# Making the KAN weights inside the forward transform stage instead of in a block of their own in front

## The reference

```
xn = group_norm(x, 32 groups)                      # no scale, no shift
x1 = spectral_conv2d(xn, w1, w2)                   # rfft2, 16 x 16 low modes of both corners mixed over channels, irfft2
y  = x1 + conv_w . xn + conv_b                     # 1x1 convolution
y  = kan_linear(y, k1_base, k1_spline, k1_scaler)  # per pixel, 64 -> 64 channels
y  = kan_linear(y, k2_base, k2_spline, k2_scaler)
out = x + gelu(y)

kan_linear(v) = silu(v) @ base.T + einsum('nik,oik->no', b_splines(v), spline * scaler[..., None])
```

## Time and profile before

| | us |
|---|---|
| median of 3 runs | 3841.19 (3837.57 to 3843.26) |
| the profiled execution | 3846.3 |
| its span | 3844.5 |
| TensorE busy | 3672.3 (96%) |
| VectorE busy | 3525.7 (92%) |
| ScalarE busy | 3397.2 (88%) |
| mean granted clock of TensorE | 0.984 |

### The profile page before, as it was taken

How to read it: one execution, slowest core, us unless ns; L and a number is a source line. 1 busy time by engine, 2 the same in 40 slices (tenths; PEclk the granted TensorE clock), 3 DMA queues, 4 the chain that set the end, 5 groups by cost and what they waited for, 6 DMA issues and landing times.

```text
span 3844.5 us, 103434 instructions
## 1 busy us (share of the span) xinstructions
PE 3672.3 (96%) x38186; PEld 1791.6 (47%) x38186; DVE 3525.7 (92%) x3959; ACT 3397.2 (88%) x3512; POOL 110.8 (3%) x132
## 2 busy tenths in 40 slices
PE   4995679999999999999999999999999999999998
PEld 2443334444444444444444444444444444444444
DVE  5773269999999999999999999999999999999997
ACT  1551269999999999999999999999999999999996
POOL 0000000000000000000000000000000000000000
PEclk9996899999999999999999999999999999999999
DMA  5999542332233223222322332232223223322321
GB/s 144 290 284 181 172 117 60 71 71 62 62 71 71 58 67 71 65 60 70 71 64 60 71 71 59 65 71 69 58 68 71 65 59 71 71 61 63 71 71 45
DMA packets 327345, 328.77 MB, mean 86 GB/s; under 512 B 87040, under 2 KB 259584, under 8 KB 325248
## 3 DMA queue, kind: packets, MB, share of 16 engines
q1 hardware_dynamic: 304256, 256.74, 24.9%
q0 software_dynamic: 18432, 67.12, 10.8%
q10 hardware_dynamic: 4608, 4.20, 0.3%
HBM read 239.90 MB, written 88.08 MB: 85 GB/s over the span
## 4 chain that ended last, share of the span: by engine, by line
PE 85%; DVE 0%; issue 0%; ACT 0%; POOL 0%; POOLq 0%; ACTq 0%; DVEq 0%
PE l_ps L1068 80%; PE y_ps L1055 3%; PE y_ps L1047 2%; DVE cube2l L944 0%; DVE cube3r L944 0%; ACT above L983 0%; ACT size L994 0%; ACT offset L998 0%; ACT S L987 0%; ACT below L991 0%; DVE cube1r L944 0%; DVE cube1l L944 0%; DVE cube0l L944 0%; ACT L987 0%; DVE cube0r L944 0%
## 5 line engine op out<-in xcount | busy, mean ns | idle before, releaser
L998 ACT ACTIVATE offset<-size 128x1024 f32<-128x1024 f32 x1280 | 1240.4, 1044 | 8.1
L944 DVE SCALAR_TENSOR_TENSOR cube0r<-below,offset 128x1024 f32<-128x1024 f32 x256 | 312.4, 1220 | 57.6 <-ACT offset L998 57.0
L1068 PE MATMUL l_ps<-S,kan_w 64*64 64x512 f32 x2048 | 357.2, 591 | 7.9 <-issue 7.9
L1068 PE MATMUL l_ps<-cube1l,kan_w 64*64 64x512 f32 x2048 | 357.1, 589 | 1.3 <-issue 1.3
L1068 PE MATMUL l_ps<-cube3r,kan_w 64*64 64x512 f32 x2048 | 356.7, 589 | 0.9 <-DVE cube3r L944 0.9
L1068 PE MATMUL l_ps<-cube0r,kan_w 64*64 64x512 f32 x2048 | 356.7, 590 | 0.6 <-DVE cube0r L944 0.6
L1068 PE MATMUL l_ps<-below,kan_w 64*64 64x512 f32 x2048 | 357.0, 591 | 0.0
L1068 PE MATMUL l_ps<-cube3l,kan_w 64*64 64x512 f32 x2048 | 356.7, 589 | 0.1
L1068 PE MATMUL l_ps<-cube2l,kan_w 64*64 64x512 f32 x2048 | 356.7, 589 | 0.1
L1068 PE MATMUL l_ps<-cube4r,kan_w 64*64 64x512 f32 x2048 | 356.7, 589 | 0.1
L1068 PE MATMUL l_ps<-cube4l,kan_w 64*64 64x512 f32 x2048 | 356.7, 589 | 0.1
(11 more groups left out here) (126 smaller groups left out, 6832.8 us busy)
## 6 DMA issues: line engine op xcount, KB each, us to landing
big<-in_x_dram SPq DMA_DIRECT2D x128, 512.0 KB, 7.0
x_ring<-in_x_dram SPq DMA_DIRECT2D x256, 256.0 KB, 4.1
act_out<-in_x_dram POOLq DMA_DIRECT2D x128, 512.0 KB, 6.8
out_dram<-act_out SPq DMA_DIRECT2D x128, 512.0 KB, 2.7
rows_scratch<-rows SPq DMA_DIRECT2D x16, 1024.0 KB, 6.1
rows_t<-rows_scratch SPq DMA_DIRECT2D x512, 32.0 KB, 5.5
big<-in_spec_w_r_dram SPq DMA_DIRECT2D x16, 512.0 KB, 11.3
big<-in_spec_w_i_dram SPq DMA_DIRECT2D x16, 512.0 KB, 11.6
```

The costliest lines, as they stand in the source:

```text
L944: nc.vector.scalar_tensor_tensor(out=cube[q][side][:], in0=distance[layer][:], scalar=EDGE - KNOTS[q], in1=offset[layer][q][:], op0=ALU.mi ...
L998: nc.scalar.activation(offset[layer][q][:], size[layer][:], ACT.Square, bias=-KNOTS[q]).then_inc(offset_ready[layer], 1)
L1068: ins = nc.tensor.matmul(dst[cols, r * MM:(r + 1) * MM], kan_w[layer][rows_, f, :], src[rows_, n * MM:(n + 1) * MM], start=(f == 0), stop= ...
```

## The change

`prepare_weights` is deleted as a block, and its work is done inside `forward`:

- SyncE loads all three tables directly behind group 0 of image 0, then the natural weights of both layers: layer 0 on partitions 0 to 63, layer 1 on 64 to 127, and the 1x1 weights on both halves, and only then groups 1 to 7. Between image 1 and the loop it issues the 1x1 bias, the inverse table and, behind a wait for VectorE, four copies of the KAN bias. In front of the mixing weights it waits for all of these.
- VectorE does the arithmetic (`spline_weights`: the body of the loop over the layers of `prepare_weights`, L244 to L288, without the clearing of `both` and the doubling of `mats`, and with its last two steps linked) once, on 128 partitions for both layers, ahead of the statistics of image 0. The working tiles lie in the third quarter of `big`.
- TensorE turns the 15 matrices (14 and the 1x1 weights) behind image 0, four to a PSUM bank, each twice for the two column halves; ScalarE evicts a bank at a time into one tile `turned_w`, in which the layers are interleaved. `kan_w[l]` and `conv_two` are views of it.
- The first iteration of ScalarE's loop over image pairs is written out.

```diff
-        kan_w = [held(f"kan_w{l}", [P, NF, C]) for l in range(2)]
-        conv_two = held("conv_two", [P, C])
+        turned_w = held("turned_w", [P, NF + 1, 2, C])
+        kan_w = [turned_w[:, 0:NF, l, :] for l in range(2)]
+        conv_two = turned_w[:, NF, 0, :]
...
 def first_half(nc, t):
-    prepare_weights(nc, t)
...
+def spline_weights(nc, dve, w, worked):
...
+    link(nc.vector.tensor_copy(m[:, F_SQUARE, :], bowl))
+    link(nc.vector.tensor_reduce(w["bias"], zero, AX.X, ALU.add))
...
 def forward(nc, t):
+        taken = [0]
+        def early(*shape):
+            n = int(np.prod(shape))
+            part = big[:, 2, taken[0]:taken[0] + n]
+            taken[0] += n
+            assert taken[0] <= C * W
+            return part if len(shape) == 1 else part.rearrange("p (a b) -> p a b", b=shape[1])
+        wide = NB + 2 * PAD
+        kan = {"spline": early(C, NB), "scaler": early(C), "padded": early(C, wide), "both": early(NK, C),
+               "inner": early(4, C), "sums": early(2, C), "mats": early(NF + 1, C), "bias": early(1)}
+        kan["diff"] = [early(C, wide - 1 - k) for k in range(PAD)]
...
+        weights_ps = [ctx.enter_context(nc.psum_tensor(f"weights_ps{i}", [P, 4, 2, C], F32)) for i in range(2)]
+        TURNS = [(f, min(f + 4, NF + 1)) for f in range(0, NF + 1, 4)]
...
         def _(sp):
             sp.dma_start(dft_h_sb[:], t["dft_h"]).then_inc(tables_loaded, 16)
             load(0, 0, 0)
             sp.dma_start(eye[:], t["ident"]).then_inc(tables_loaded, 16)
+            sp.dma_start(dft_w_sb[:], t["dft_w"]).then_inc(tables_loaded, 16)
+            for l, (b_, s_, c_) in enumerate(((t["k1_base"], t["k1_spline"], t["k1_scaler"]),
+                                              (t["k2_base"], t["k2_spline"], t["k2_scaler"]))):
+                own = slice(l * C, (l + 1) * C)
+                sp.dma_start(kan["spline"][own], s_).then_inc(natural_loaded, 16)
+                sp.dma_start(kan["scaler"][own], c_).then_inc(natural_loaded, 16)
+                sp.dma_start(kan["mats"][own, F_SILU, :], b_).then_inc(natural_loaded, 16)
+                sp.dma_start(kan["mats"][own, NF, :], t["conv_w"]).then_inc(natural_loaded, 16)
             for k in range(1, N_GRP):
                 load(0, 0, k)
-            sp.dma_start(dft_w_sb[:], t["dft_w"]).then_inc(tables_loaded, 16)
             for k in range(N_GRP):
                 load(1, 1, k)
+            for d in range(2):
+                sp.dma_start(t["conv_bias"][d * C:(d + 1) * C, :],
+                             t["conv_b"].rearrange("(c a) -> c a", a=1)).then_inc(consts_loaded, 16)
+            sp.dma_start(t["inv_w_sb"][:], t["inv_w"]).then_inc(consts_loaded, 16)
+            sp.wait_ge(mats_ready, 1)
+            for l in range(2):
+                for d in range(2):
+                    sp.dma_start(t["kan_b"][l][d * C:(d + 1) * C, :],
+                                 kan["bias"][l * C:(l + 1) * C]).then_inc(consts_loaded, 16)
             with sp.Fori(1, B // 2) as b2:
...
+            sp.wait_ge(consts_loaded, 112)
             for part in range(2):
                 load_mix_weights(sp, t, weights[:, 2 + part], 0, part)
...
         def _(dve):
+            nc.vector.memset(kan["padded"], 0.0).then_inc(padded_clear, 1)
+            dve.wait_ge(padded_clear, 1)
+            dve.wait_ge(natural_loaded, 128)
+            spline_weights(nc, dve, kan, worked)
+            dve.sem_inc(mats_ready, 1)
             image(0, 0, 0)
...
         def _(pe):
             image(0, 0, 0, before=False)
+            pe.wait_ge(mats_ready, 1)
+            for n, (f0, f1) in enumerate(TURNS):
+                if n >= 2:
+                    pe.wait_ge(weights_kept, n - 1)
+                for f in range(f0, f1):
+                    for d in range(2):
+                        ins = nc.tensor.matmul(weights_ps[n % 2][d * C:(d + 1) * C, f - f0, :, :].rearrange("i l o -> i (l o)"),
+                                               kan["mats"][:, f, :], eye[:], start=True, stop=True,
+                                               tile_position=(0, d * C))
+                ins.then_inc(weights_turned, 1)
...
         def _(act):
-            with act.Fori(0, B // 2) as b2:
+            image(0, 0)
+            for n, (f0, f1) in enumerate(TURNS):
+                act.wait_ge(weights_turned, n + 1)
+                nc.scalar.activation(t["turned_w"][:, f0:f1, :, :], weights_ps[n % 2][:, 0:f1 - f0, :, :],
+                                     ACT.Copy).then_inc(weights_kept, 1)
+            image(1, 1)
+            with act.Fori(1, B // 2) as b2:
                 for par in range(2):
                     image(2 * b2 + par, par)
```

More of the change, by code:

```diff
@@ L31 @@
 NF = 4 + 2 * NK
+PAD = ORDER + 1
 NS = MODES + 1
@@ L342, in forward @@
         along_w_done, modes_kept = sem("along_w_done"), sem("modes_kept")
+        natural_loaded, consts_loaded, padded_clear = sem("natural_loaded"), sem("consts_loaded"), sem("padded_clear")
+        worked, mats_ready = sem("worked"), sem("mats_ready")
+        weights_turned, weights_kept = sem("weights_turned"), sem("weights_kept")
         seen_by_sp = sem("forward_seen_by_sp")
@@ L566, in _ @@
                 rows = slice(i * C, (i + 1) * C)
-                ins = nc.tensor.matmul(ps_bias[i][rows, :], conv_two[rows, :], pair_rm[rows, :], start=True, stop=True,
+                ins = nc.tensor.matmul(ps_bias[i][rows, :], conv_two[rows], pair_rm[rows, :], start=True, stop=True,
                                        tile_position=(i * C, i * C))
@@ L929, in prepare @@
                 for i in range(2):
-                    nc.vector.tensor_scalar(conv_t[par][:, i * C:(i + 1) * C], conv_two[:],
+                    nc.vector.tensor_scalar(conv_t[par][:, i * C:(i + 1) * C], conv_two,
                                             image_rs[:, bass.ds(2 * pair + i, 1)], None, ALU.mult).then_inc(conv_ready, 1)
```

161 lines of the change are left out of this document (45 added, 116 removed).

## The result

| | before | after |
|---|---|---|
| median, in the runs beside the prediction | 3842.23 us (4 runs) | 3799.98 us (4 runs, 3796.32 to 3803.37) |
| median, once more, in five rounds later on | 3840.34 us (7 runs) | 3803.79 us (4 runs, 3799.69 to 3807.03) |
| the profiled execution | 3846.3 | 3802.6 |
| its span | 3844.5 | 3800.8 |

The ratio of after to before is 0.9896 (95% interval 0.9884 to 0.9908), and 0.9909 (0.9893 to 0.9926) in the repetition: faster, by 42 us and by 37 us, about 1%, with neither interval reaching 1. The forecast was 3800.2.

The account below looks back on a forecast made before the run. The image stream was taken as DMA-bound to its last image, the tile stage as TensorE-bound and untouched. -47.55 + 4.45 + 2.5 - 0.4 = -41.0 us, from 3841.2 to 3800.2 us; range 3792 to 3811.

Parts of the forecast that it names:

- The block in front, -47.55: Start of the program: forward's first issue moves from 48.42 to 0.87 us, and the whole shift is passed on.
- Nine added issues ahead of group 1, +4.45: SyncE, image 0: nine issues at 0.64 us add 5.74, less 0.93 and 0.36, together +4.45 us.
- Seven small transfers, +2.5: SyncE between image 1 and image 2: seven at 0.36 us each, +2.5 us; bounds 0 and 12.2.
- The price of 0.36: Cost in us per small transfer inside the image stream, taken from the delay of arrivals by the 64 KB column table.
- SyncE's wait, 0: SyncE before the bias copies: weights ready at 21.8 us, SyncE there at 33.6; 12 us of cover, cost 0.
- VectorE late for image 0, 0: Image 0's statistics start at 21.8 us instead of about 5.6, still early enough for images 2 and 3; cost 0.
- the reserve of 4.4 us: Image 15's licence from statistics: TensorE starts earlier, slack goes from -0.4 to +4.4 us, so a 0.4 us wait goes.
- rival 1: Image stream: the seven small transfers drain it, costing 12.2 us instead of 2.5; 3809.9 us, chance 0.12.
- rival 2: Image 0: TensorE may stay at its lower clock level and be late; middle 3809 us, chance 0.05.
- rival 3: Front of forward: added issues hide, the seven cost nothing, the whole 47.55 us is gained; 3793.6 us, chance 0.07.
- rival 4: Tile stage: weight loads slow down reading interleaved layers; at 3 ns more each 3886 us, slower than before; chance 0.03.
- rival 5: Front of the program: nothing gained, as the chain doesn't run through it; 3841 us, chance 0.01.

Follow-up runs that it names:

- experiment 2: Kernel after, with the preparation moved back to a block in front that still does both layers at once on 128 partitions; 3824.24 us, ratio 0.9954.
- experiment 3: Kernel after, with the eight natural weight loads issued by ScalarE at its start instead of by SyncE; 3806.12 us.
- experiment 4: Kernel after, with the seven small constant transfers issued by ScalarE, three at its start and four behind its evictions of the turned weights; 3803.08 us.
- experiments 6 and 7: Kernel after, with VectorE's weight arithmetic done twice in a row (6) or four times (7); 3801.61 us and 3827.31 us.
- experiment 9: Kernel before, with the first iteration of ScalarE's loop over image pairs in forward written out; 3839.14 us.
- experiment 1: Kernel before, with the table for the transform along w loaded ahead of groups 1 to 7 of image 0; 3840.15 us, ratio 0.9998.
- experiments 5 and 11: One version run twice: kernel after, with eight natural loads and seven constants issued by ScalarE, SyncE issuing only tables and images; 3797.32 us and 3795.94 us.

## Why the prediction was right, point by point

- *The block in front, -47.55.* Right to the hundredth, and experiment 2 shows the principle at another length.
- *Nine added issues ahead of group 1, +4.45.* When SyncE has issued image 1 it is 32.53 us behind its first issue (33.40 - 0.87), against 28.27 before (62.27 + 8 x 1.80 - 48.42): +4.3. The working called this issue time only, with the bytes moved while SyncE issues, and the rows agree: DMA is at 0.27 of its measure from 6 to 9 us. The bytes cost something only when the loads run beside the images, as in experiment 3.
- *Seven small transfers, +2.5.* This is the term that was mis-sized. The loop starts 6.03 us later for them and its 112 loads and end are done in 200.5 us instead of 202.05, the forecast's 0.4 us of wait among that: net +4.5, or +4.9 without the 0.4. Taken away alone they gave back 3.9 (experiment 4). The fixed cost of 2.0 us that the prediction quotes from the Trainium skill, "DMA: Bandwidth & Descriptors", section "Anatomy of one DMA", is given there for DMAs that GpSimd issues, and these are SyncE's; the runs have 4 to 5 us for the seven and not the 14 of its estimate. The price of 0.36 was read from a single small load with full transfers behind it; seven in a row use up the lead that SyncE has over the landings, and then each costs its issue.
- *Sum of these:* -47.55 + 4.3 + 4.5 = -38.8 at the mark, where the forecast had -41.0. The two medians say -42.3 and -36.6. That the time after fell within 0.3 us of 3800.2 is chance: the 2.2 us short at the mark were covered by the scatter of the stages behind it. The repetition, 3803.79 us, missed by 3.6.
- *SyncE's wait, 0.* Right: no such wait in the trace, cover forecast 12 us, measured 15 (experiments 6 and 7).
- *VectorE late for image 0, 0.* Right: statistics began at 21.31 (21.8 forecast), and 12 us later still in experiment 6 without cost.
- *TensorE, and the reserve of 4.4 us.* Right in sign, far too small. The statistics of image 13 began at 210.78 us in the profile after, so the licence for image 15's first group is there at 212.2, and the transfer is issued at 39.43 + 104 x 1.79 = 225.6: 13.4 us of reserve (the row stands below this list). The turns took 3.54 us and not 6, the seven transfers held the stream and not TensorE, and the missing table loads made 0.63 us per pair of images (experiment 9). As DMA bounds the stage this reserve brought no time. (At its upper bound for the turns the prediction has 3804.4 us. By its own terms, a wait of 4.6 instead of none, it is 3804.8.)
- *The rivals.* The stream did run dry (rival 1), at 4 to 5 us and not 12. TensorE did start at its lower clock (rival 2): the two matmuls of a group took 1.97 to 1.98 us at 6.70, 12.30 and 15.25 and 1.08 at 18.11, so the low level lasted three groups and not eight, and the reserve hid it. (The level is read from these durations; the column of the granted clock says 1.00 from 6 to 9 us.) In front of group 1 TensorE had waited 3.6 us for DMA, but it was slow before that wait too, so these rows cannot say that a wait brings the lower clock. The inverse rows stage can. In the profile of before the granted clock was 1.00 from 439.4 to 444.4 us and 0.52 in the next 5 us, around the end of a wait for DMA of 3.02 us; around one of 3.10 us it stayed at 1.00 in experiment 1. The Trainium skill, "TensorE: Matmul & The Clock Gate", section "HAM oscillation", says that waits for DMA inside a loop bring the lower clock; the first of these profiles agrees and the second does not. Group 1 could not be issued past the others (rival 3). Weight loads stayed at 133 ns (rival 4). The gain is there (rival 5 is out).

VectorE's statistics of image 13, kernel after:

```profile
210.78 10.53 DVE L355 BATCH_NORM_STATS2 stats<-big 128x256 f32 x32
```

## What to carry to other kernels

A stage that is full on DMA is the place for preparation that used to stand in front: here 12 us more of VectorE work inside it cost nothing, while each microsecond in front of the first bulk transfer cost one. Keep small transfers out of the queue that feeds the stream, and price them by count: one costs little, but a row of seven cost its issue time, 0.6 to 0.7 us each, once the lead of the issuer was used up. For effects of a few microseconds in a run of 3800, compare a mark in the trace that repeats to 0.3 us rather than medians of four runs that differ by 3.8 for one kernel; and look at what scatters behind the mark before a stage is called the cause of a difference.

## What I had not expected of the hardware

- TensorE's granted clock in the inverse rows stage took one of two courses in two executions of one and the same kernel, 88.3 and 83.6 us for the stage (experiments 5 and 11); 12 of 13 profiles fall to one or the other. With waits for DMA of about 3 us in both, the granted clock in the profile of before is 0.76 to 0.93 in each 10 us from 429 to 469 us, and in experiment 1 it is full from the second pair of images on.
- The head of ScalarE's loop carried a function table load of 1.28 us in every iteration (8 in the stage). With one iteration written out in front, one load was left. The same function is used throughout, so it is the place of the load and not a change of function.
- Loads of 16 to 128 KB issued from another queue beside the image stream still took their share: with eight of them 15 images took 2.3 us longer to issue (experiment 3).
